# Weighted values of the third group of heads placed directly in front of those of the fourth

## What is computed

```python
x = x + attention(layernorm(x))       # 16 heads of 8 features, stablemax3 in place of softmax
x = x + experts(layernorm(x))         # router, best 2 of 4 experts, 512 hidden, silu(a) * b

attn = einsum('bhsd,bhtd->bhst', q, k) * scale
attn = stablemax3(attn)               # s(logits - row maximum) / sum; s is a cubic, or its inverse below 0
out  = einsum('bhst,bhtd->bhsd', attn, v)
```

## Time and profile before

| | |
|---|---|
| runs | 1126.56, 1124.47, 1125.14 us, median 1125.14 |
| profiled execution | span 1123.6 us; its time outside the span is not listed |
| TensorE matmul busy | 1101.5 us, 98% |
| TensorE weight load busy | 934.8 us, 83% |
| ScalarE busy | 1003.9 us, 89% |
| VectorE busy | 979.8 us, 87% |
| GpSimd busy | 750.0 us, 67% |
| granted TensorE clock | 0.998 of full speed |

### The profile page before, as it was taken

How to read it: one execution, slowest core, us unless ns; L and a number is a source line. 1 busy time by engine, 2 the same in 40 slices (tenths; PEclk the granted TensorE clock), 3 DMA queues, 4 the chain that set the end, 5 groups by cost and what they waited for, 6 DMA issues and landing times.

```text
span 1123.6 us, 29304 instructions
## 1 busy us (share of the span) xinstructions
PE 1101.5 (98%) x9968; PEld 934.8 (83%) x9968; DVE 979.8 (87%) x1789; ACT 1003.9 (89%) x1034; POOL 750.0 (67%) x999
## 2 busy tenths in 40 slices
PE   6989999999999999999999999999999999999998
PEld 5768888888888888888888888888888888888888
DVE  5789999999899899989999999989989899998844
ACT  1799999999999999999999999999999999999982
POOL 4547766777676687776677767668777667776530
PEclk9999999999999999999999999999999999999999
DMA  6343433233333223443223343332333322333000
GB/s 190 110 143 119 127 104 94 92 110 120 124 113 99 90 90 121 123 123 106 90 86 115 118 126 113 95 95 90 122 123 121 108 88 87 117 119 124 30 6 11
DMA packets 130383, 117.49 MB, mean 105 GB/s; under 512 B 15748, under 2 KB 124964, under 8 KB 130340
## 3 DMA queue, kind: packets, MB, share of 16 engines
q1 hardware_dynamic: 128004, 113.78, 32.7%
q10 hardware_dynamic: 2336, 3.15, 0.8%
HBM read 94.18 MB, written 21.09 MB: 103 GB/s over the span
## 4 chain that ended last, share of the span: by engine, by line
PE 91%; DVE 3%; ACT 3%; ACTq 1%; issue 1%; DMA 0%; POOL 0%; SPq 0%; POOLq 0%; DVEq 0%
PE banks L1301 33%; PE banks L1576 20%; PE sc L1387 11%; PE banks L1319 10%; PE sc L1559 3%; PE misc L1301 2%; PE banks L1610 2%; DVE mx L994 1%; PE misc L1434 1%; PE misc L1412 1%; PE misc L1452 1%; PE banks L1559 1%; ACT poly L768 1%; PE sc L1301 1%; DVE poly L909 1%; PE banks L1295 1%
## 5 line engine op out<-in xcount | busy, mean ns | idle before, releaser
L481 POOL TENSOR_TENSOR hid<-hid,gate_all 128x512 f32<-128x512 f32 x240 | 378.6, 1638 | 157.8 <-DMA gate_all<-gate_scratch 130.8
L909 DVE SCALAR_TENSOR_TENSOR poly<-w_sq,sc 128x1024 f32<-128x1024 f32 x252 | 303.6, 1215 | 36.5 <-ACT w_sq L659 36.4
L1301 PE MATMUL banks<-xn_hi,w_hi 128*128 128x256 f32 x976 | 289.3, 296 | 0.2
L1301 PE MATMUL banks<-xn_lo,w_hi 128*128 128x256 f32 x976 | 275.2, 282 | 0.0
L1301 PE MATMUL banks<-xn_hi,w_lo 128*128 128x256 f32 x976 | 274.4, 281 | 0.0
L659 ACT ACTIVATE w_sq<-sc 128x1024 f32<-128x1024 f32 x252 | 255.6, 1029 | 10.3 <-PE sc L1387 6.4
L768 ACT ACTIVATE poly<-poly,two 128x2048 f32<-128x2048 f32 x128 | 252.1, 1991 | 0.4
L1576 PE MATMUL banks<-w_sb,hid 128*128 128x128 f32 x1920 | 245.9, 281 | 0.2 <-POOL hid L481 0.2
L1576 PEld LDWEIGHTS banks<-w_sb,hid 128*128 128x128 f32 x1920 | 223.3, 191 | 16.3 <-POOL hid L481 0.4
L773 ACT ACTIVATE poly<-poly 128x2048 f32<-128x2048 f32 x128 | 236.8, 1895 | 0.0
L994 DVE TENSOR_REDUCE mx<-sc 128x4 f32<-128x1024 f32 x192 | 229.4, 1212 | 6.5 <-PE sc L1559 5.7
(11 more groups left out here) (186 smaller groups left out, 1367.3 us busy)
## 6 DMA issues: line engine op xcount, KB each, us to landing
qk_scratch<-qk_split SPq DMA_DIRECT2D x32, 512.0 KB, 3.1
q_pad<-qk_scratch SPq DMA_DIRECT2D x256, 64.0 KB
k_tile<-qk_scratch SPq DMA_DIRECT2D x124, 128.0 KB, 2.6
q_tile<-qk_scratch SPq DMA_DIRECT2D x124, 128.0 KB, 2.5
k_stack<-qk_scratch SPq DMA_DIRECT2D x124, 128.0 KB
gate_all<-gate_scratch SPq DMA_DIRECT2D x30, 512.0 KB, 4.5
x_in<-in_L_attn_x_dram SPq DMA_DIRECT2D x32, 128.0 KB, 2.1
x_res<-in_L_attn_x_dram SPq DMA_DIRECT2D x32, 128.0 KB, 2.3
```

The lines of the kernel that those rows point to most:

```text
L481: nc.gpsimd.tensor_tensor(h, h, by_token.unsqueeze(1).to_broadcast([128, 2, C, 128]), ALU.mult).then_inc(gated, 1)
L909: nc.vector.scalar_tensor_tensor(poly[:, u, :], w_sq[:, u % 2, :], 3.0, distance_buf(n, u), ALU.add, ALU.mult).then_inc(poly_ok, 1)
L1301: last = nc.tensor.matmul(dst, lhs[a], rhs[b], start=(k == 0), stop=(k == len(terms) - 1))
```

## The change

In a settled first half, `weighted_values` of group 2 is issued directly in front of that of group 3, so behind `distance(1)` (not for n = 2, where the step before still issued it). In the second half it is issued only in the last step; in all others the second half ends with `up_b_unit` of unit 0, directly behind `queries_and_keys`. Semaphores, their counts, buffers and all other engines' orders are as before.

```diff
--- before.py
+++ after.py
@@ -1457,6 +1457,8 @@
                     values()
                     distance(0)
                     distance(1)
+                    if not (isinstance(i, int) and n == 2):
+                        weighted_values(i, off - 1, 2)
                     weighted_values(i, off - 1, 3)
                     ups(1)
                     distance(2)
@@ -1670,8 +1672,8 @@
                         up_b_unit(i, off - 1, 0)
                         late_up_a(LATE, 1)
                         late_up_b(LATE, 1)
-                    weighted_values(i, off, 2)
-                    if not (isinstance(i, int) and n == B - 1):
+                        weighted_values(i, off, 2)
+                    else:
                         up_b_unit(i, off - 1, 0)
                     return
```

## The result

The changed kernel takes 1136.77 us (median of 4 runs, 1135.98 to 1137.88), the kernel before 1124.95 (4 runs): ratio 1.0103, 95% interval 1.0091 to 1.0115. The forecast was 1137.4 us. The spans of the two profiled executions, 1135.6 and 1123.6 us, differ by 12.0.

The account below looks back on a forecast made before the run. TensorE's issue time was taken to bound the kernel. 12 steps x 0.47 + 16 x 0.37 + 0.7 = 12.3 us, added to 1125.14, gave 1137.4 us; own range 1133 to 1142, 8-in-10 range 1128 to 1143.

Parts of the forecast that it names:

- TensorE's issue time is the step: Steady loop: a microsecond more or less of TensorE's own issue time is a microsecond of the some 33 us step.
- The merge saves 0.32 us: Groups 2 and 3 in a row: 0.14 + 0.18 us less TensorE work per pair, 9.3 us over 29 pairs.
- rival 4: Moved pair: products don't merge, a second 1.00 instead of 0.86 adds 4 us, 1141.5 us; chance within the forecast's.
- The copy holds `values()`, then the transfer holds `distance(0)`: After `queries_and_keys`: VectorE's copy stalls `values()` 0.23 us, then the maxima's transfer lets `distance(0)` start only 0.39 us earlier.
- The transfer's price: Maxima's transfer, from SP's issue to the start of `distance(0)`: taken as 3.05 us, bounds 2.1 and 3.44.
- Nothing downstream gives it back: Behind the moved pair: TensorE waits for nobody until the next `maxima_T`, so the delay is carried to it.
- The copy's stall: In front of `values()`: waiting for VectorE's copy of queries and keys costs 0.23 us.
- rival 1: At `distance(0)`: transfer lands early, the copy sets the start; 0.09 us faster per step, 1122.5 us; chance 0.11.
- same: Whole kernel: no change, meaning within 0.2% (2.3 us) of the time before; chance 0.11.
- Rival 2: Steady step: VectorE's and ScalarE's ring sets its length, TensorE's stall is paid elsewhere, 1125 us; chance 0.11.
- Rival 3: Maxima's transfer takes 3.44 us with the store moving behind it; each pair costs 0.86, 1150 us; chance 0.08.
- The two rules: Maxima's transfer: skill page gives two DMA engines for two destination partitions, and a fit estimating 2.1 us for 32 KB.

Follow-up runs that it names:

- the kernel without waits: Changed kernel with `distance(0)` waiting for the previous step's maxima transfer and the copy cut to 32 of 512 columns: 1119.04 us, ratio 0.9942.
- the first experiment: Changed kernel with `distance(0)` waiting for the maxima transfer of the step before: 1125.05 us; same edit on the kernel before as control: 1124.53 us.
- the kernel with the first row early: Changed kernel, queries and keys earlier, one transfer per row, the first issued as soon as VectorE has made that row: 1123.95 us, ratio 0.9989.
- half of the change alone: Kernel before with group 2 moved only behind `up_b_unit`, not merged with group 3: 1125.39 us, ratio 1.0001.

## Why the prediction was right

**TensorE's issue time is the step.** Right for time that is added: the chain of the kernel before was TensorE's without a break, and 29 stalls of under half a microsecond net made 10.9 us. For time taken away it holds only in part: of 0.32 us less in a step, 0.19 came through. The prediction had "more or less" count alike.

**The merge saves 0.32 us.** Right in place: 5.54 to 5.22 us between issue and first up projection, once both waits are gone. But I would have credited it with 9.3 us, and the kernel without waits gained 6.6, of which 0.19 us a step, 5.6 us, are the steps: `polynomial(0)`, fed by ScalarE's stream, stands some 0.2 us behind the first limit. That the two groups merge (rival 4) shows in the 1.86 us of the pair.

**The copy holds `values()`, then the transfer holds `distance(0)`.** Both seen in the trace after, and in this order. The transfer's price, 3.05 us from two waits at the edges of the loop, was the term on which the sign hung; the odd steps have 3.05, the even ones 2.95. Why they differ by 0.1 us stays open. The even steps lost part of the advantage again: their distances take 1.12 us to the pair, not 1.10. Their sum is 2.95 + 1.12 + 1.86 = 5.93 against 3.54 + 1.10 + 1.00 = 5.64, +0.29 where I had +0.37; the odd ones 3.05 + 1.09 + 1.86 = 6.00 against 5.54, +0.46 where I had +0.47.

**Nothing downstream gives it back.** Right for the steps: ScalarE's waits for the up projections rose from 39.6 to 51.2 us in total, so ScalarE only waits longer. In the last step more came back than I had counted: 0.4 us of the 0.86 are left, not 0.7.

**What was luck.** The sum came to 12.3 us, the profiles differ by 12.0 and the medians by 11.8. But the moved pairs account for 10.9 of the 12.0, 1.4 less than the sum: the 12 even steps from n = 4 to 26 were priced at 0.37 and measure 0.29, and the last step was priced at 0.7 and measures 0.4. The 1.1 us of a slower clock at the start of one profile, which the prediction knew nothing of, fill most of the gap. The direction and the size of the steps don't rest on that.

**What was off.** The copy's stall: 0.33 us, not 0.23, since `values()` took some 0.1 us more to the next start behind the stall (0.47, not 0.37). It was hidden behind the transfer, so the forecast didn't feel it; but rival 1 was priced with it. Had the transfer landed early, the change would have been no change (1125.05 us in the first experiment), not a gain of 2.6 us. Its chance belonged to "same". Rival 2 fell with the result, though its ring of ScalarE and VectorE is what ended the gain of the faster kernels. Rival 3 fell with the steady landing, the same with the store behind it (3.05) as without (3.09 for n = 1 in the profile after).

**The two rules weighed.** The share of the DMA engines was 0.14 while the data went to two partitions, and 0.30 to 0.33 with one destination row of 8 pieces per transfer, which landed 0.8 us sooner behind its own issue. The Trainium skill ("DMA: Bandwidth & Descriptors", "Why a DMA increments its semaphore by 16 and not by 1") lets the slowest dimensions of both sides set the number of engines; for a row of 8 pieces out of 32 partitions that gives an estimated eight engines, a share of 0.5. The trace agrees for two partitions; for the row it agrees in direction, at about five engines' worth. The fit in its section "Anatomy of one DMA — SWDGE (gpsimd) path" gives an estimated 2.1 us for the transfer; it is made for another way of issuing, and the measured 3.05 decides.

## What to carry to other kernels

Work that stands between an issue and the wait for it is not free to move, even where the trace shows no wait there: before moving it, add up what is left in the gap and compare it with the landing, taken from the one place in the trace where that very transfer was waited for. Merging small pieces with like ones saves their changeover (here 0.32 us of 1.2), but look for the place where the merged piece still fills the gap. And with three engines close together, a gain of the first ends where the next takes over, here after 0.2 us of 33. Last, before a difference of two profiles is put down to a change, look where it arises: here 1.1 of 12.0 us stood in front of the first instruction moved.

## What the runs showed of the hardware

- A transfer of 32 KB between on-chip tiles into two partitions took 2.9 to 3.1 us from issue to the waiting matmul; cut into one transfer per partition, the second one took 2.2 to 2.3 from its own issue to the matmul (from n = 5 to 27, in the kernel with the first row early), with the same bytes per row; in n = 29 of the same kernel it took 3.44.
- A group of 16 matmuls with 32 columns of weights takes 1.00 us to the next start, two in a row 1.86, and the first six full-width matmuls behind it 0.90 instead of 0.71.
- The four 128x128 matmuls of `values()` take 0.47 us to the next start behind a stall (first experiment) and also, without a stall, directly behind a group with 32 columns of weights (half of the change alone); behind full-width matmuls in a stream they take 0.36 to 0.37.
- The same instructions reached the issue for n = 2 at 82.9, 83.9 or 85.2 us; the granted clock from 20 to 40 us was 1.00, 0.91 and 0.83 in these profiles.
